# Recurrent attention: the heads' biases of a chunk of decays are subtracted on GpSimd, and ScalarE takes one exponential of 1024 columns

## The reference, cut to what matters

```python
logfg = jax.nn.log_sigmoid(f_pre)
Fcum = jnp.cumsum(logfg, axis=-1)
Dmat = Fcum[..., :, None] - Fcum[..., None, :] + i_pre[..., None, :]
Dmat = jnp.where(causal, Dmat, -jnp.inf)
m = jnp.max(Dmat, axis=-1, keepdims=True)
Smat = jnp.exp(Dmat - m)
qk = jnp.einsum('bhsd,bhtd->bhst', q, k) / jnp.sqrt(jnp.float32(dqk))
C = qk * Smat
n = jnp.maximum(jnp.abs(jnp.sum(C, axis=-1, keepdims=True)), jnp.exp(-m))
h = jnp.einsum('bhst,bhtd->bhsd', C / n, v)
```

## Time and profile before

| | before |
|---|---|
| median of 3 runs | 809.64 us (809.07 to 810.78) |
| the profiled execution's own time | 809.85 us |
| its span in the profile | 808.1 us |
| PE busy | 721.6 us, 89% |
| DVE busy | 518.1 us, 64% |
| ACT busy | 376.0 us, 47% |
| POOL busy | 126.5 us, 16% |
| the 128 exponentials of L647 | 39.0 us of ACT, 394 ns each |

### The profile page before, as it was taken

How to read it: one execution, slowest core, us unless ns; L and a number is a source line. 1 busy time by engine, 2 the same in 40 slices (tenths; PEclk the granted TensorE clock), 3 DMA queues, 4 the chain that set the end, 5 groups by cost and what they waited for, 6 DMA issues and landing times. The chain is left out here.

```text
span 808.1 us, 10609 instructions
## 1 busy us (share of the span) xinstructions
PE 721.6 (89%) x4038; PEld 599.5 (74%) x4038; DVE 518.1 (64%) x938; ACT 376.0 (47%) x781; POOL 126.5 (16%) x114
## 2 busy tenths in 40 slices
PE   1889999879999999999999999997579999999956
PEld 1768888667877789876888778875467888878845
DVE  4726566963875557555666447645438978889783
ACT  4767677553744425443344333343455354553321
POOL 5033353510000010000100001000121302223010
PEclk9979999979999999999999999999599999999978
DMA  4066443000000000000000000500000000000000
GB/s 169 2 186 229 126 129 95 1 1 0 1 1 1 2 0 1 1 1 1 1 1 0 1 1 1 209 1 0 1 0 1 1 26 1 26 1 1 27 0 27
DMA packets 21282, 25.75 MB, mean 32 GB/s; under 512 B 976, under 2 KB 19408, under 8 KB 20464
## 3 DMA queue, kind: packets, MB, share of 16 engines
q1 hardware_dynamic: 20576, 23.76, 8.8%
q10 hardware_dynamic: 656, 1.31, 0.4%
HBM read 22.91 MB, written 2.16 MB: 31 GB/s over the span
## 5 line engine op out<-in xcount | busy, mean ns | idle before, releaser
L1113 DVE TENSOR_TENSOR h_raw<-h_s,bank 128x512 f32<-128x512 f32 x104 | 71.3, 686 | 150.4 <-ACT h_s L1103 132.2
L1103 ACT ACTIVATE h_s<-bank 128x512 f32<-128x512 f32 x104 | 62.1, 597 | 186.1 <-PE bank L91 186.1
L1118 DVE TENSOR_TENSOR h_ring_lo<-h_raw,h_ring_hi 128x512 fp32r<-128x512 f32 x104 | 77.0, 740 | 0.1
L1107 ACT ACTIVATE h_ring_hi<-h_raw 128x512 fp32r<-128x512 f32 x104 | 64.7, 622 | 0.2 <-DVE h_raw L1113 0.2
L90 PE MATMUL bank<-fused_lo,h_ring_hi 128*128 128x256 f32 (+1 forms) x224 | 62.6, 280 | 0.0
L89 PE MATMUL bank<-l_xT_hi,l_wgu 128*128 128x512 f32 x128 | 52.5, 410 | 7.9 <-DVE l_h L2043 5.6
L89 PE MATMUL bank<-f_yT_hi,mlp_hi 128*128 128x512 f32 x128 | 52.5, 410 | 3.0 <-DVEq L1531 3.0
L89 PE MATMUL bank<-f_xT_hi,ffn_hi 128*128 128x512 f32 (+2 forms) x120 | 47.9, 399 | 7.7 <-DVE f_xT_lo L1568 7.1
L90 PE MATMUL bank<-l_xT_lo,l_wgu 128*128 128x512 f32 x128 | 51.0, 398 | 0.0
L91 PE MATMUL bank<-l_xT_hi,l_lo 128*128 128x512 f32 x128 | 50.9, 398 | 0.0
L91 PE MATMUL bank<-f_yT_hi,fused_lo 128*128 128x512 f32 x128 | 50.8, 397 | 0.0
(11 more groups left out here) (310 smaller groups left out, 2072.0 us busy)
## 6 DMA issues: line engine op xcount, KB each, us to landing
m_W<-m_scratch SPq DMA_DIRECT2D x16, 512.0 KB, 5.9
fused_raw<-in_fused SPq DMA_DIRECT2D x1, 3584.0 KB, 15.9
res<-in_x SPq DMA_DIRECT2D x4, 512.0 KB, 6.1
fused_raw<-in_fused SPq DMA_DIRECT2D x2, 1024.0 KB, 8.1
l_raw<-in_layer SPq DMA_DIRECT2D x1, 2048.0 KB, 10.3
out_x<-res SPq DMA_DIRECT2D x16, 128.0 KB, 1.8
l_raw<-in_layer SPq DMA_DIRECT2D x1, 1280.0 KB, 12.7
fused_raw<-in_fused SPq DMA_DIRECT2D x1, 1120.0 KB, 5.7
```

The source lines that it names most:

```text
L1103: self.nc.scalar.activation(self.s[u % 2][r, :], gate[r, :], ACT.Silu).then_inc(self.silu.sem, 1)
L1107: self.nc.scalar.activation(self.unit(i, u)[0], self.product(i, u), ACT.Copy).then_inc(self.hi.sem, 1)
L1113: self.nc.vector.tensor_tensor(out=self.product(i, u), in0=self.s[u % 2][r, :], in1=up[r, :], op=ALU.mult).then_inc(self.hidden.sem, 1)
L1118: self.nc.vector.tensor_tensor(out=lo, in0=self.product(i, u), in1=f32(hi), op=ALU.subtract).then_inc(self.lo.sem, 1)
```

## The change

POOL gets one more instruction for each chunk, ahead of its selection: it subtracts `tg`, spread along the 128 queries of each head, from the whole 128x1024 tile. A new semaphore, `m_shiftedW`, stands between the subtraction and the selection. The first subtraction also waits for ACT's copy of `tg` (`TG_IN`). ACT then takes one exponential of 1024 columns with no bias, in place of 8 with a bias.

```diff
@@ mlstm_phase
+    shifted_W = one("m_shiftedW")
@@ scalar: weights(n)
                 act.wait_ge(masked.sem, n + 1)
-                w = W[n % RING]
-                for h in range(H):
-                    last = nc.scalar.activation(w[:, h, :], w[:, h, :], ACT.Exp, bias=tg[:, c, b * H + h:b * H + h + 1], scale=-1.0)
-                last.then_inc(weight.sem, 1)
+                w = W[n % RING][:, :, :].rearrange("p h s -> p (h s)")
+                nc.scalar.activation(w, w, ACT.Exp, scale=-1.0).then_inc(weight.sem, 1)
@@ gpsimd: mask_weights(n)
-                w = W[n % RING]
+                w, (b, c) = W[n % RING], divmod(n, C)
                 pool.wait_ge(loaded[n % RING], 16 * (n // RING + 1))
+                nc.gpsimd.tensor_tensor(out=w[:, :, :], in0=w[:, :, :], in1=expand(tg[:, c, of(b)], P), op=ALU.subtract).then_inc(shifted_W, 1)
+                pool.wait_ge(shifted_W, n + 1)
                 nc.gpsimd.affine_select(out=w[:, :, :], in_=w[:, :, :], compare_op=ALU.is_ge, fill=1e30,
                                         base=0, pattern=[[0, H], [1, P]], channel_multiplier=-1).then_inc(masked.sem, 1)
@@ gpsimd: before the loop
                 roots(b)
+            pool.wait_ge(act_tables, TG_IN)
             mask_weights(0)
```

## The result

| | before | changed |
|---|---|---|
| median | 809.46 us (809.07 to 810.78, 4 runs) | 817.85 us (816.64 to 819.60, 4 runs) |
| the profiled execution's own time, its span | 809.85, 808.1 us | 816.64, 814.6 us |
| mean granted clock of the span | 0.962 | 0.958 |

The ratio of changed to before is 1.0108, with a 95% interval of 1.0091 to 1.0126: 8.4 us slower, where 4.2 was forecast. A second set of runs of the changed kernel (experiment e13) gave 1.0092, 1.0064 to 1.0120. In e3, e4, e11 and e15 one execution of each was disturbed (931 to 2444 us); the ratios leave it out.

The account below looks back on a forecast made before the run. The PE was taken as the bound in the attention's steady part, DVE in its tail. ACT 0, start 0, and three DVE-POOL collisions gave 3.0 to 5.8 us, taken as 4.2: 813.8 us against 809.64, range 809.5 to 816.8.

Parts of the forecast that it names:

- ACT gains nothing: In the attention, ACT's 22 us less work over 16 chunks is worth 0, hidden by the PE's own work.
- faster rival: In the attention, ACT released `evict` and splits; three or four evictions come 0.4 to 0.5 us sooner, 808.0 us; chance 0.08.
- What POOL pays: Per chunk, a subtraction of 1.94 us, 2.0 with semaphore, 32 us in all; on POOL's list alone it costs nothing.
- rival with 2.4: On POOL, the subtraction takes 2.4 us; start 0.3 us late, three places longer, 7.2 us in all, 816.8 us; chance 0.10.
- The start costs nothing: Before the first inverse root, POOL's masks end at 70.4, the root waits for DVE until 72.89; 2.5 us left.
- `normal_x` is blocked: At three places, DVE's four TENSOR_SCALARs stand still beside POOL's subtraction and mask; the forecast case, 4.2 us, chance 0.60.
- the rival that it isn't: At three places, `normal_x` runs beside the subtraction; 0.1 us each, 809.9 us, no change; chance 0.22.
- together or alternate: First place: DVE's four `normal_x` instructions pass together (0.9 us more PE wait) or alternate with POOL's (1.8 us).
- The path to the PE: Mean square, inverse root, `norm`, `turn_h`, `low_h`: delay past 1.1 us of slack enters the PE's wait, 0.9 to 1.8 us.
- The sign that I had named for this path: The PE's wait for `low_h` in the attention goes up from 7.2 us by 2 to 4 us.
- The sum: ACT 0, start 0, first two places 0.9 to 1.8 each, third 1.2 to 2.2: 3.0 to 5.8 us, taken as 4.2.
- The clock: In the attention, the PE was read at full clock in 120 to 140 us; the sum gave its clock no term.

Follow-up runs that it names:

- e13: Changed kernel, unaltered, run again with more executions; 816.07 us, ratio 1.0092.
- e3: Changed kernel with `normal_x` of sequences 0 to 2 moved to where POOL is idle or in an inverse root; 813.34 us, ratio 1.0046.
- e4: Kernel before with `normal_x` of sequences 0 to 2 moved as in e3, as a control; 809.25 us, ratio 0.9995.
- e11: e9 with four BN_STATS of 256 columns as stand-ins in the three old places of `normal_x`; 813.64 us, ratio 1.0044.
- e15: Changed kernel with the subtraction for the first six chunks only; 810.09 us, ratio 1.0011.
- e1: Kernel before with only ACT's part, one exponential of 1024 columns without a bias, no subtraction; 809.53 us, ratio 0.9999.
- e16: Changed kernel with the subtraction for chunks 6 to 15 only; 817.31 us, ratio 1.0092.
- e10: Kernel before with all four `normal_x` moved behind `gate_rows()`; 807.98 us, ratio 0.9995.
- e8: Changed kernel with two memsets of the tile in place of each subtraction; 814.30 us, ratio 1.0084.
- e18: Changed kernel, unaltered, profiled a third time; 817.40 us.
- e2: Changed kernel with the subtraction kept but eight exponentials of 128 columns without a bias; 816.06 us, ratio 1.0083.
- e17: Kernel before, unaltered, profiled once more; 806.85 us.
- e6: Changed kernel with `normal_x` moved at the third place only; 812.67 us, ratio 1.0051.
- e7: Changed kernel with `normal_x` moved at the first two places only; 816.52 us, ratio 1.0083.
- e5: Repeat of e3, the changed kernel with `normal_x` moved at all three places, for a readable profile; 813.72 us, ratio 1.0063.
- e12: e9 with the second mask of a turn moved behind the second inverse root for the first two sequences; 812.91 us, ratio 1.0042.
- e9: Changed kernel with all four `normal_x` moved behind `gate_rows()`; 812.78 us, ratio 1.0053.

## Why the prediction was wrong

**ACT gains nothing: right.** The exponential takes 1.056 us (1.04 forecast) and e1 is at 0.9999. In the changed kernel the time became waiting: between 40 and 165 us ACT's `evict` waits 26.9 us for the PE's L485 where it waited 9.2. The faster rival is ruled out.

**What POOL pays: right.** The subtraction takes 1.90 us (1.94 forecast), so the rival with 2.4 is out. On POOL's list alone the second root would be in time: its second mask ended at 84.42, ahead of the root's old place at 84.89, and POOL then waited 2.34 us for DVE.

**The start costs nothing: right**, by luck in part, in the profile (72.92 against 72.89), and e15 and e16 don't contradict it for the medians. It holds only where the PE's half clock at 53 to 60 us holds the first root back to 72.9; by my own sum POOL is through at 70.4, and a start with more clock has that root due at 69.44 (e10). This too was the clock taken as given.

**`normal_x` is blocked: right**, and the rival that it isn't is out: 1.99 us for one, and e11 shows that it is the kind of instruction that matters; no run isolates its two-port form as the reason, but e8, e11 and `weigh_scores` all agree with it. Of "together or alternate" it was alternate, in the order that I had written down: one, the subtraction, one, the mask, two. The mean square started at 84.82, where that case had 85.7.

**The path to the PE: wrong in its detail.** I let the delay run from the mean square through the inverse root and `norm` to `low_h`, with 1.1 us of slack. With the root at 86.76 that path would have cost 0.8 us at the first place. The PE stalled earlier, on `add`, which I had left out because nothing waited for it in the trace of before; that gave 1.6. The sign that I had named for this path, 2 to 4 us more of waiting for `low_h`, didn't come (6.8 us against 7.2). The sum hardly noticed: the root-to-root intervals show about 1.6, 1.35 and 1.45 us at the three places, **4.40 us together, where the sum said 3.0 to 5.8 and took 4.2**.

**The clock: the step that failed.** The sum had no term for it. I read the clock of 140 to 160 us as 1.00 in the earlier trace rows and took the PE's speed there as given. In all five profiles in which the full subtraction meets `normal_x` at all three places (changed, e13, e18, e2, e16) the PE ran part of that window at 1.2 GHz, and the tail took 147.9 to 148.7 us, against 145.5 to 146.8 in five of the six profiles without a collision there (before, e17, e4, e10, e15). The sixth, e1, lost some clock as well (0.91) and its tail is as long, 147.97, with no collision at all. So 3 to 10 us more at half clock in 140 to 180 us cost about 2 to 2.5 us here, and what the change does is to make them likely. e6 and e7 point to the third collision as what does so. That this stall in itself lowers the clock wasn't shown: e5, e11 and e12 have no blocked TENSOR_SCALAR there and still 0.91.

The account for the first set of medians, 8.4 us: 4.4 blocked DVE work, 2.0 clock in the tail, 0.3 the time around the span (816.64 − 814.6 against 809.85 − 808.1), together the 6.8 between the two profiled executions; the other 1.6 is that the changed kernel's profiled execution was the lowest of its four and before's lay 0.4 above its median. In which stretches the other executions lose it, no trace shows, but each execution's mean clock is on record, and that this remainder goes with the clock can be read from it. The changed kernel's four have 0.952 to 0.958, the 94 of the kernel before in the experiments' sets a median of 0.964. At equal clock most of the second half is gone:

| mean clock of the execution | span before | span changed (e2 and e13 included) |
|---|---|---|
| 0.958 | 810.5, 810.6 | 814.6, 815.5 |
| 0.960 | 808.8 to 810.2 (11) | 814.7 |
| 0.961 | 808.1, 808.2 (5) | 812.4, 812.4 |

That leaves 4.0 to 5.9 us, about what stands between the roots, and the kernel before alone goes from 804.3 to 805.1 us at 0.967 to 810.5 at 0.958. So about half of the loss is the lists and half is time at half clock; why the change brings more of it stays **open**. So does a small remainder of e9, which at equal clock (0.962) is 1.4 to 2.5 us above before, with 1.2 us between the roots. With a half-clock term of 2 to 2.5 us the forecast would have been about 816; the range, which had no room for it, ended at 816.8.

## What to carry to other kernels

Before work goes to GpSimd, list what VectorE executes beside it: here a long GpSimd instruction stopped `normal_x`'s TENSOR_SCALARs whether it read or only wrote SBUF, and the instructions with two operands in SBUF if it read, and a chain of short ones got one turn per GpSimd instruction. The price is not proportional: half the subtraction cost 0.1 us, the whole 4.4, since the slack is spent first, and that slack has to be taken over every user of the delayed list, also those that nothing waits for yet (`add`). Where a new stall lands in a tail in which the engines wait for one another anyway, put a term for the PE's clock into the sum and into the range, and before comparing two kernels compare executions of equal mean clock.

## What the runs showed of the hardware beyond that

- POOL also waits for DVE: the subtraction at 81.13 takes 2.06 us instead of 1.90, the only one above 1.9 in its group, because a TENSOR_SCALAR was first.
- One ACTIVATE of 1024 columns without a bias takes 1.056 us, and eight of 128 took 2.44. On an engine that waits anyway this factor of 2.3 was worth nothing.
- The same program loses the PE's clock at different points of the tail: from about 148.6 to 158.9 us in one profile, from 155.7 to 165.9 in another, with all inverse roots up to 153.93 in the same places to 0.05 us.
